# GNN with a mixture of experts on one Trainium2 core: the first 14 slices of the adjacency build among the preparation

## Chip, cores and metric

One Trainium2 chip (trn2), one of its NeuronCores. The metric is the device time of one execution in microseconds (us), and the number compared is the median of several runs.

## What is computed

The input is `x`, 3125 nodes of 256 features, and 53125 directed edges (25000 drawn pairs in both directions, one self loop per node), sorted by destination. It goes through a graph network and a mixture of experts, each with a residual:

```python
h = layernorm(x)
for _ in range(6):                                   # six steps
    r = maximum(h @ W1.T + b1, 0)
    msg = segment_sum((r @ W2.T + b2)[src], dst)     # over 53125 edges
    xr, xz, xn = split(msg @ W_ih.T + b_ih)          # GRU cell
    hr, hz, hn = split(h @ W_hh.T + b_hh)
    z = sigmoid(xz + hz)
    h = (1 - z) * tanh(xn + sigmoid(xr + hr) * hn) + z * h
x = x + h
y = layernorm(x)
logits = y @ Wg + bg + bias                          # 8 experts, the best 2
x = x + sum over the two of weight * (relu(y @ F1[e] + fb1[e]) @ F2[e] + fb2[e])
```

## The kernel before, in words

**Data.** The segment sum is a product with the dense adjacency matrix `adj`, 25 tiles of 128 source nodes by 3136 destination columns in fp8, which stays in SBUF. States and ReLU outputs are kept as a high and a low fp16 part (`x_hi`, `x_lo`; `r_hi`, `r_lo`), and the gate weights too (`wht`, `wct`; the latter is W_ih times W2, one product less in each step).

**Preparation.** The edges come sorted in blocks of 64. VectorE turns them into keys and rows; TensorE transposes them and spreads the lowest and highest destination of each block over the partitions (`diag`, `lim_b`). From these VectorE works out for each slice of 16 columns the first block (`bnd[.., 0]`) and the last block (`bnd[.., 1]`) (L643 to L653); the first goes on to `slot_key` and `picked` and a product on TensorE (L1473) that fetches each slice's edges as three slots of 128. The last block serves only the question whether a slice has more edges than three slots hold (`more`, and `bound` with its two DMAs), which decides the `slow_flag`. With it set, `redo` code and exact steps run on every engine, in branches that are skipped otherwise; these inputs skip them. Then come the statistics of x (L675, L678), `rstd` as a power on GpSimd (L503), x normalised on VectorE (L735), its transposes on TensorE with their halves made by ScalarE and VectorE (`state_part`, 13 of them), W1, the product W_ih times W2 (L1514), and eight transposes of scaled gate weights (L1530).

**Build.** `adj` has 196 slices in 7 turns of 28. For each slice VectorE compares (`hots`, L889 and L895: one `hot_row` for two slices, three `hot_key`), TensorE multiplies (`slice_sums`, L1637: three matmuls into one of two banks), ScalarE evicts to fp8 (`evict`, L1280) and GpSimd copies two slices into `adj` (L506). A turn ends with the node degrees (L1645). The engines each run their own written order. What they do between the slices stands in the functions `beside(w, b)`, where b is the slice's place in its turn: turn 0 holds the first nine ReLU sums of step 0 (b = 0, 3, 6 ...), turn 1 four more and the first messages, later turns messages and gates of the window of the turn before. VectorE may be four slices ahead of TensorE (`DEEP`).

**Steps.** Step 0 is fused into the build. Then TensorE reads the flag and runs steps 1 to 4 in a loop and step 5 written out, seven windows of up to 512 columns each: messages (L1587), gates (L1611); a step's last window shares its time with the next step's ReLU sums (`step_end`). At the start of step 1 ScalarE issues the DMAs that reload x and the router's weights for the tail (L1344 to L1351), as soon as GpSimd has cleared `x1` (L515).

**Experts.** The tail adds the residual, normalises, chooses the experts and scatters rows of 260 floats to `slot_in` in DRAM; an expert loop over tiles of 256 rows multiplies, and GpSimd adds each result to `out` with an indirect DMA (L591). At the end of each expert GpSimd waits for its two DMAs (L595, L596, the `tock` operations).

**The order around the change.** All orders are written by hand, with semaphores. Until now no slice starts before the eighth weight transpose and the last state part are done (L1535 to L1537). The lines that set the place of a slice in the preparation, for TensorE:

```python
pe.wait_ge(sem("w_lo"), 9)
pe.wait_ge(sem("slot_tables"), 1)
pe.wait_ge(sem("state_lo"), NW)
...
for g in range(NSL):
    slice_sums(g)
    beside(g // GROUP - 1, g % GROUP)
```

## Time and profile before

| | |
|---|---|
| median of 3 runs | 1967.47 us (1966.49 to 1970.06) |
| the profiled execution's own time | 1965.98 us |
| its span in the trace | 1964.2 us |
| busy share of the span | TensorE 93%, its weight loads 56%, VectorE 56%, ScalarE 31%, GpSimd 17% |
| mean granted TensorE clock | 0.969 of full speed |
| instructions | 30148 |

All engine times below are counted from the start of the span. PE is TensorE, PEld its weight loads, DVE VectorE, ACT ScalarE, POOL GpSimd, SP SyncE. A granted clock of 1.0 is 2.4 GHz, 0.5 is 1.2 GHz. "128x512 f16<-128x512 f32" is partitions by elements of output and input. In brackets stands how long an engine was idle before an instruction, and what ended the wait; "issue" means that the engine waited for nothing that the profile shows. A duration in a timeline can overlap with the next one's start; the cost of an instruction in a full queue is the distance of two starts.

### The profile page before, as it was taken

The numbers are of one execution on the slowest core, as the hardware profiler recorded it, in microseconds if no ns is written. First come the engines' busy times: TensorE is split into PE (matmuls) and PEld (weight loads), VectorE is DVE, ScalarE is ACT, GpSimd is POOL, SyncE is SP. The second block draws the span as 40 slices with busy tenths as digits, with TensorE's granted clock in tenths as the row PEclk, the third lists the DMA queues.
The fourth block names the chain that finished last, engine by engine and source line by source line (L and its number), as shares of the span: only waits on it lengthen the run. The fifth ranks groups of instructions, "written<-read, shape, count | busy, mean of one in ns | idle before, by whom it ended". The sixth has DMA issues, their size and how long they took to land.

```text
span 1964.2 us, 30148 instructions
## 1 busy us (share of the span) xinstructions
PE 1825.1 (93%) x10716; PEld 1097.3 (56%) x10717; DVE 1103.2 (56%) x2622; ACT 608.8 (31%) x1254; POOL 337.3 (17%) x454
## 2 busy tenths in 40 slices
PE   2789999999999999999999999999999999839996
PEld 1555555555444574445744457444574456629996
DVE  6897888875144562344624446244452556736775
ACT  0154444434112242122411224122241112216663
POOL 1011111100455500000000000000000013234665
PEclk7799999999999999999999999999999999959998
DMA  8940000000443300000000000000000011564543
GB/s 265 336 158 2 1 2 2 1 2 2 166 133 133 129 23 1 1 1 1 2 1 1 1 1 2 1 1 1 1 1 1 12 44 56 218 247 73 87 74 52
DMA packets 74505, 109.64 MB, mean 56 GB/s; under 512 B 12334, under 2 KB 65369, under 8 KB 73076
## 3 DMA queue, kind: packets, MB, share of 16 engines
q1 hardware_dynamic: 51086, 49.57, 8.1%
q0 software_dynamic: 18368, 38.09, 7.7%
q10 hardware_dynamic: 4902, 20.01, 2.6%
q8 instruction: 92, 1.51, 0.3%
q14 instruction: 57, 0.47, 0.1%
HBM read 43.59 MB, written 65.05 MB: 55 GB/s over the span
## 4 chain that ended last, share of the span: by engine, by line
PE 72%; issue 14%; POOL 7%; DVE 5%; ACT 1%; DMA 0%; POOLq 0%; SPq 0%; ACTq 0%; DVEq 0%
PE bank L1587 36%; PE bank L1611 25%; PE bank L1562 5%; PE bank L1637 4%; POOL out L591 3%; POOL slot_in L568 2%; POOL tick L590 1%; DVE hot_key L895 1%; PE bank L1473 1%; ACT stage L1280 1%; DVE xa L735 0%; DVE hot_row L889 0%; POOL rstd L560 0%; PE bank L1514 0%; DMA out<-slot_y,dest 0%
## 5 line engine op out<-in xcount | busy, mean ns | idle before, releaser
L1587 PE MATMUL bank<-adj,r_hi 128*128 128x512 fp8e4 (+4 forms) x2100 | 731.1, 353 | 0.0
L1587 PE MATMUL bank<-adj,r_lo 128*128 128x512 fp8e4 (+4 forms) x2016 | 703.3, 353 | 0.0
L1587 PEld LDWEIGHTS bank<-adj,r_hi 128*128 128x128 f16 x2100 | 205.9, 98 | 188.4 <-issue 1.9
L1587 PEld LDWEIGHTS bank<-adj,r_lo 128*128 128x128 f16 x2016 | 197.6, 98 | 179.8 <-issue 1.9
L792 DVE SCALAR_TENSOR_TENSOR m_lo<-bank,msg_unit,m_hi 128x512 f16<-128x512 f32 (+4 forms) x84 | 57.2, 682 | 283.4 <-ACT m_hi L1210 283.1
L1611 PE MATMUL bank<-x_hi,wht_hi 128*128 128x512 f16 (+4 forms) x504 | 177.3, 352 | 0.5 <-DVE m_lo L792 0.5
L1611 PE MATMUL bank<-m_hi,wct_lo 128*128 128x512 f16 (+4 forms) x504 | 177.3, 352 | 0.0
L1611 PE MATMUL bank<-x_hi,wht_lo 128*128 128x512 f16 (+4 forms) x504 | 177.3, 352 | 0.0
L1611 PE MATMUL bank<-m_lo,wct_hi 128*128 128x512 f16 (+4 forms) x504 | 177.3, 352 | 0.0
L1611 PE MATMUL bank<-m_hi,wct_hi 128*128 128x512 f16 (+4 forms) x504 | 177.3, 352 | 0.0
L1611 PE MATMUL bank<-x_lo,wht_hi 128*128 128x512 f16 (+4 forms) x504 | 177.3, 352 | 0.0
L1210 ACT ACTIVATE m_hi<-bank,msg_unit 128x512 f16<-128x512 f32 (+4 forms) x84 | 53.1, 632 | 352.3 <-PE bank L1587 352.3
L895 DVE TENSOR_SCALAR hot_key<-iota_key,slot_key 128x400 f16<-128x400 f16 x588 | 156.5, 325 | 0.0
L1280 ACT ACTIVATE stage<-bank 128x400 fp8e4<-128x400 f32 x196 | 98.5, 504 | 153.9 <-PE bank L1637 147.2
L1637 PE MATMUL bank<-hot_key,hot_row 128*128 128x400 f16 x588 | 126.8, 334 | 12.4 <-DVE hot_key L895 7.1
L555 POOL MEMSET x_rows<- 128x4 f32 (+1 forms) x3 | 0.2, 97 | 793.1 <-PE bank L1794 793.1
L1217 ACT ACTIVATE gate_a<-gate_a,gate_bias,gate_unit 128x512 f32<-128x512 f32 (+4 forms) x84 | 63.7, 759 | 228.5 <-DVE gate_a L808 228.5
L1221 ACT ACTIVATE gate_a<-gate_a,gate_bias,gate_unit 128x512 f32<-128x512 f32 (+4 forms) x84 | 63.6, 757 | 150.4 <-DVE gate_a L822 150.4
L811 DVE SCALAR_TENSOR_TENSOR gate_z<-degree,deg_w,bank 128x512 f32<-128x512 uint16 (+4 forms) x84 | 56.8, 676 | 89.2 <-PE bank L1611 89.2
L506 POOL COPY adj<-stage 128x200 uint32<-128x200 uint32 x98 | 46.7, 477 | 319.8 <-ACT stage L1280 319.8
L591 POOL DMA_INDIRECT out<-slot_y,dest x58 | 90.9, 1568 | 20.5 <-issue 14.4
L785 DVE SCALAR_TENSOR_TENSOR r_lo<-bank,r_hi 128x512 f16<-128x512 f32 x72 | 49.2, 689 | 80.4 <-ACT r_hi L1204 79.4
(298 smaller groups left out, 2878.9 us busy)
## 6 DMA issues: line engine op xcount, KB each, us to landing
slot_in<-fill_rows SPq DMA_DIRECT2D x2, 13520.0 KB, 68.9
ffn_scratch<-pair POOLq DMA_DIRECT2D x32, 512.0 KB, 3.2
ffn_w<-ffn_scratch ACTq DMA_DIRECT2D x8, 2048.0 KB, 18.8
x_rows<-in_L_ffn_W POOLq DMA_DIRECT2D x32, 256.0 KB, 4.0
slot_x<-slot_in SPq DMA_DIRECT2D x30, 260.0 KB, 3.1
xa<-in_x SPq DMA_DIRECT2D x1, 3072.0 KB
x<-in_x ACTq DMA_DIRECT2D x1, 3072.0 KB
out<-x SPq DMA_DIRECT2D x4, 512.0 KB
```

The lines of the kernel that those rows point to most:

```text
L591: pool.indirect_dma_start(out[:], bass.IndirectOffsetOnAxis(ap=dest[j][:, 0:1], axis=0), slot_y[j][:], None, bounds_check=N - 1, oob_is_er ...
L792: v.scalar_tensor_tensor(m_lo[:, w % 2, f, 0:n], bank[f][:, 0:n], msg_unit[:, 0:1], m_hi[:, w % 2, f, 0:n], ALU.mult, ALU.subtract)\
L811: ins = v.scalar_tensor_tensor(z, dg, deg_w[:, 2 + f:3 + f], bank[5][:, 0:n], ALU.mult, ALU.add)
L895: last = v.tensor_scalar(hot_key[k][:], iota_key[:], slot_key[:, g, s:s + 1], None, ALU.is_equal)
L1210: a.activation(m_hi[:, w % 2, f, 0:n], bank[f][:, 0:n], ACT.Copy, scale=msg_unit[:, 0:1]).then_inc(sem(again + "msg_hi"), 1)
L1217: a.activation(gate_a[:, 0:n], gate_a[:, 0:n], ACT.Sigmoid, bias=gate_bias[:, f:f + 1], scale=gate_unit[:, f:f + 1]).then_inc(acts, 1)
L1221: a.activation(gate_a[:, 0:n], gate_a[:, 0:n], ACT.Tanh, bias=gate_bias[:, 4 + f:5 + f], scale=gate_unit[:, 4 + f:5 + f]).then_inc(acts, 1)
L1280: a.activation(stage[g // 2 % 2][:, :, (b % 2) * SW:(b % 2 + 1) * SW], bank[2 + (g + i) % RING][:, 0:NT * SW].rearrange("p (q c) -> p q c" ...
L1562: last = mm(o[:, k * D:(k + 1) * D], xs[:, t, n0:n0 + P], ws[:, t, :], start=False, stop=True, skip_group_check=True)
L1587: last = mm(bank[f][:, 0:n], r[:, q, f * P:(f + 1) * P], c, start=q == 0 and i == 0, stop=q == NT - 1 and i == len(todo) - 1)
L1611: last = mm(bank[b][:, 0:n], wgt, mov, start=i == 0, stop=i == len(todo) - 1)
L1637: last = mm(bank[2 + (g + i) % RING][:, 0:NT * SW], hot_row[b // 2 % 2][:, b % 2, s, :], hot_key[k][:], start=s == 0, stop=s == SLOTS - 1)
```

## The change

1. **Slices in the preparation** (`AHEAD = 14`). Slices 0 to 13 are built between the state parts and the weight transposes, in the written orders of TensorE, VectorE and ScalarE. As `adj` lies over memory that the preparation still uses, their evictions go to seven buffers of their own (`early_stage`), which GpSimd copies once states and weights are done. The state parts use banks 0 and 1 instead of 2 and 3, the transposes of W_hh wait for the three scaled parts of wc and for `deg_w`.
2. **ReLU sums of turn 0** stand at slices 14, 16, 17, 19, 20, 22, 23, 25, 26 instead of 0, 3, ... 24, and their low parts four slices later.
3. **x is normalised by ScalarE** with scale `rstd` and bias `shift`, a new VectorE operation behind `rstd`: twelve tiles ahead of W1's copies, the others among the slices.
4. **Out of VectorE's head**: the copies to `key_t`, `row_t` and of the upper limits go to ScalarE; the last blocks (`last_block`) go behind slices 56 and 57, `bound` and `more` (`bounds`) behind slice 58. `block_id` and `mask` are fp16 now, one mask for each half.
5. **SyncE** sends the bounds after the seven `adj` copies of the twin rows, and it issues the reload DMAs, once in the slow branch and once in a new branch for the common case.
6. **TensorE's branches**: the redo code moves into the slow branch of the steps, and the common branch stands first.
7. **GpSimd** waits for the last output DMAs once, after the last expert, instead of after each.

The diff, cut to its core (a line of dots stands for what is left out: what only moved along, or is told in the list):

```diff
+X_FIRST = 12
+AHEAD = 14
+RELU_AT = (14, 16, 17, 19, 20, 22, 23, 25, 26)
@@ SyncE @@
+            for w in range(TURNS):
...
             sp.wait_ge(sem("bound_col"), 1)
...
-            for w in range(TURNS):
+            def reload():
+                sp.wait_ge(sem("x1_clear"), 1)
...
+            with sp.If(slow < 1):
+                reload()
@@ GpSimd @@
             for p in range(NSL // 2):
+                if p == 0:
+                    pool.wait_ge(sem("state_lo"), NW)
+                    pool.wait_ge(sem("w_lo"), 9)
                 pool.wait_ge(sem("stage_full"), 2 * p + 2)
...
-                for j in range(TT):
-                    pool.wait_ge(sem(f"y_out{j}"), pool.snap(pool.snap(done) * 16 + 16))
-                    pool.tensor_tensor(tock[:, e * TT + j:e * TT + j + 1], valid[:], valid[:], ALU.mult).then_inc(sem("expert_sent"), 1)
+            for j in range(TT):
+                pool.wait_ge(sem(f"y_out{j}"), pool.snap(pool.snap(done) * 16 + 16))
+                pool.tensor_tensor(tock[:, j:j + 1], valid[:], valid[:], ALU.mult).then_inc(sem("expert_sent"), 1)
@@ VectorE @@
+            dve.wait_ge(sem("rstd_ready"), 1)
+            v.scalar_tensor_tensor(shift[:], mv[:, :, 0], -1.0, rstd[:], ALU.mult, ALU.mult).then_inc(sem("shift_ready"), 1)
             v.memset(ones_h[:], 1.0)
...
-            for t in range(NT):
-                v.tensor_scalar(xa[:, t, :], xa[:, t, :], mv[:, t, 0:1], rstd[:, t:t + 1], ALU.subtract, ALU.mult)\
-                 .then_inc(sem("x_norm"), 1)
...
+            def last_block(t):
+                link(v.scalar_tensor_tensor(mask[t][:, 0:NB], block_id[:, 0:NB], 1.0, mask[t][:, 0:NB], ALU.add, ALU.mult))
+                link(v.tensor_reduce(bnd[:, t, 1:2], mask[t][:, 0:NB], AX.X, ALU.max))
...
+                if w == 1 and b in (0, 1):
+                    last_block(b)
+                if w == 1 and b == 2:
+                    bounds()
...
+            hots(0)
...
+            state_part(0)
+            for u in range(1, X_EARLY):
+                state_part(u)
+                hots(u)
+            for c in range(3):
+                dve.wait_ge(sem("wc_sums"), c + 1)
+                v.tensor_reduce(peak[:, 1, 2 * c:2 * c + 2], bank[4 + c][:].rearrange("p (o j) -> p o j", o=2), AX.X, ALU.max, apply_absolute_value=True).then_inc(sem("peaks"), 1)
+                hots(X_EARLY + c)
...
+            hots(X_EARLY + 3)
             for i, wt in enumerate((wht, wct)):
                 for j in range(4):
...
+                    if X_EARLY + 4 + 4 * i + j < AHEAD:
+                        hots(X_EARLY + 4 + 4 * i + j)
-            for g in range(NSL):
+            for g in range(AHEAD, NSL):
@@ ScalarE @@
+            def normalise(t):
+                a.activation(xa[:, t, :], xa[:, t, :], ACT.Identity, bias=shift[:, t:t + 1], scale=rstd[:, t:t + 1]).then_inc(sem("x_norm"), 1)
+            act.wait_ge(sem("shift_ready"), 1)
+            for t in range(X_FIRST):
+                normalise(t)
...
+            state_part(0)
+            state_part(1)
+            for u in range(2, X_EARLY):
+                evict(u - 2)
+                normalise(X_FIRST + 2 * (u - 2))
+                normalise(X_FIRST + 2 * (u - 2) + 1)
+                state_part(u)
...
+                    if X_EARLY + 2 + 4 * i + j < AHEAD:
+                        evict(X_EARLY + 2 + 4 * i + j)
...
-            act.wait_ge(sem("stage_free"), NSL // 2)
-            act.wait_ge(sem("x1_clear"), 1)
@@ TensorE @@
+            state_part(0)
+            for u in range(1, X_EARLY):
+                state_part(u)
+                slice_sums(u - 1)
...
             for c in range(3):
...
                 last.then_inc(sem("wc_sums"), 1)
+                slice_sums(X_EARLY - 1 + c)
...
+                    pe.wait_ge(sem("deg_w_done"), 1)
...
+                    if X_EARLY + 2 + 4 * i + j < AHEAD:
+                        slice_sums(X_EARLY + 2 + 4 * i + j)
...
-            with pe.If(slow > 0):
+            def redo_first():
...
-            with pe.If(slow > 0):
-                all_steps(True)
             with pe.If(slow < 1):
                 all_steps(False)
+            with pe.If(slow > 0):
+                redo_first()
+                all_steps(True)
```

## Rows read from the trace of the kernel before

**Rows 1.** Stretches: us, each engine's busy time (instructions), PEclk, DMA share, GB/s.

```profile
66.90:82.90 16.00, 4.70 (x24) 3.84 (x25) 13.58 (x36) 3.14 (x6) 0.00 (x0) 0.68 1.09 336
...
91.70:105.50 13.80, 9.68 (x58) 8.51 (x57) 11.88 (x26) 7.36 (x16) 0.00 (x0) 0.75 1.10 336
105.50:142.30 36.80, 32.00 (x214) 20.55 (x215) 34.53 (x115) 19.61 (x65) 6.32 (x14) 0.95 0.39 142
```

**Rows 2.** VectorE in the table chain, timeline and groups by shape.

```profile
24.75 2.22 DVE L639 COPY lim_b<-bank 128x512 f32<-128x512 f32 x4 [2.16 <-PE bank L1460]
...
L651 DVE SCALAR_TENSOR_TENSOR e_f<-block_id,mask 128x831 f32<-128x831 f32 x2 | 2.0, 1025 | 0.1
L652 DVE TENSOR_REDUCE bnd<-e_f 128x1 f32<-128x831 f32 x2 | 2.0, 1019 | 0.1
...
40.19 0.17 DVE L655 CAST bound<-bnd 128x4 int32<-128x4 f32 x1
```

**Rows 3.** rstd on GpSimd and what VectorE does then; the x normalisation.

```profile
57.13 4.36 POOL L503 TENSOR_TENSOR rstd<-rstd,expo 128x25 f32<-128x25 f32 x1 [50.90 <-DVE rstd L680]
...
60.85 0.17 DVE L700 MEMSET ones_h<- 128x128 f16 x1
...
L735 DVE TENSOR_SCALAR xa<-xa,mv,rstd 128x256 f32<-128x256 f32 x25 | 8.2, 405 | 0.0
```

**Rows 4.** ScalarE, timeline at 1707 us: start, duration, operation.

```profile
1707.69 0.65 ACT L1217 ACTIVATE gate_a<-gate_a,gate_bias,gate_unit 128x310 f32<-128x310 f32 x1 [3.71 <-DVE gate_a L808]
1708.24 0.63 ACT L1219 ACTIVATE gate_z<-gate_z,gate_bias,gate_unit 128x310 f32<-128x310 f32 x1
```

**Rows 5.** VectorE, timeline in turn 0: two slices' keys, relu_lo, hot_row.

```profile
114.52 1.48 DVE L895 TENSOR_SCALAR hot_key<-iota_key,slot_key 128x400 f16<-128x400 f16 x6
115.92 0.68 DVE L785 SCALAR_TENSOR_TENSOR r_lo<-bank,r_hi 128x512 f16<-128x512 f32 x1
116.52 0.65 DVE L889 TENSOR_TENSOR hot_row<-iota_row,turn_row 128x768 f16<-128x768 f16 x1
```

**Rows 6.** TensorE, timeline in turn 0: one slice, one ReLU sum, two slices.

```profile
111.97 0.68 PE L1637 MATMUL bank<-hot_key,hot_row 128*128 128x400 f16 x3 [0.18 <-ACT stage L1280]
112.48 0.38 PE L1557 MATMUL bank<-b_rows,ones_h 128*128 128x256 f16 x2
...
114.01 1.18 PE L1637 MATMUL bank<-hot_key,hot_row 128*128 128x400 f16 x6
```

**Rows 7.** TensorE, timeline: four transposes of x in the preparation.

```profile
97.11 1.06 PE L1484 MATMUL bank<-ident,xa 128*128 128x128 f32 x4
```

**Rows 8.** Line 506: durations in ns, least, median, most.

```profile
L506 POOL COPY adj<-stage x98: 356/357/1078, 112.0 to 427.6; 128x200 uint32<-128x200 uint32 x98
```

**Rows 9.** Turn 2's start, timelines of VectorE and TensorE.

```profile
185.28 0.67 DVE L792 SCALAR_TENSOR_TENSOR m_lo<-bank,msg_unit,m_hi 128x448 f16<-128x448 f32 x1
...
187.21 0.35 PE L1611 MATMUL bank<-x_hi,wht_hi 128*128 128x448 f16 x1
```

**Rows 10.** TensorE after steps 0 and 1, timelines; and the stretch between.

```profile
493.19 0.18 PE L1731 MATMUL bank<-ones_h 128*128 128x2 f16 x1 [6.35 <-issue]
...
493.61 0.63 PE L1587 MATMUL bank<-adj,r_lo 128*128 128x512 fp8e4 x1
494.04 0.63 PE L1587 MATMUL bank<-adj,r_hi 128*128 128x512 fp8e4 x1
...
738.75 0.17 PE L1731 MATMUL bank<-ones_h 128*128 128x2 f16 x1 [1.59 <-issue]
...
494.00:496.00 2.00, 2.00 (x6) 0.76 (x5) 0.02 (x1) 0.00 (x0) 0.00 (x0) 0.50 0.05 12
```

**Rows 11.** The end: TensorE before the last columns; VectorE's last slot_y, GpSimd's tick.

```profile
1717.60 1.41 PE L1759 MATMUL bank<-ident,x_rows 128*128 128x128 f32 x6 [4.73 <-DVE x_rows L1042]
...
1951.02 0.34 DVE L1146 TENSOR_SCALAR slot_y<-y_sum,share 128x256 f32<-128x256 f32 x1
...
1952.74 0.19 POOL L590 TENSOR_TENSOR tick<-valid 128x1 f32<-128x1 f32 x1
```

More of the change, by code:

```diff
@@ L189, in gnn_ffn @@
         at_messages = used[0]
+        early_scope = ExitStack()
+        yb = allocator(early_scope)
+        early_stage = [yb(f"early_stage{p}", [P, NT, 2 * SW], F8) for p in range(AHEAD // 2)]
+        skip_to(yb, "to_gate_z", at_messages + 5 * DT * 1024)
+        mask = [yb("mask0", [P, CG * P], F16)]
+        skip_to(yb, "to_x_new", at_messages + 6 * DT * 1024)
+        block_id = yb("block_id", [P, CG * P], F16)
+        mask.append(yb("mask1", [P, CG * P], F16))
+        early_end = used[0]
+        early_scope.close()
         m_hi = ss("m_hi", [P, 2, DT, 512], F16)
@@ L196, in gnn_ffn @@
         at_build = used[0]
+        assert edge_end <= at_messages + 5 * DT * 1024 and early_end <= at_build
         bs = ExitStack()
@@ L357, in columns_of, with staged @@
             return (FUSED_LEN[w], FUSED_COL[w]) if fused else (WIN_LEN[w], WIN_COL[w])
+        def staged(p):
+            return early_stage[p] if p < AHEAD // 2 else stage[p % 2]
         def ring_free(engine, item):
@@ L628, in _ @@
             last.then_inc(sem("diags"), 1)
-            dve.wait_ge(sem("keys_t"), 1)
-            for i, table in ((0, key_t), (1, row_t)):
-                for h in range(2):
-                    last = v.tensor_copy(table[:, h * 2 * P:(h + 1) * 2 * P], bank[2 * i + h][:].rearrange("p (c two) -> p c two", two=2)[:, :, 0])
-            last.then_inc(sem("edge_table"), 1)
             dve.wait_ge(sem("lims_b"), 1)
-            for m in range(2):
-                for h in range(2):
-                    n = min(4, CG - 4 * h) * P
-                    last = v.tensor_copy(lim_b[:, m, h * 512:h * 512 + n], bank[4 + 2 * m + h][:, 0:n])
+            for h in range(2):
+                n = min(4, CG - 4 * h) * P
+                last = v.tensor_copy(lim_b[:, 0, h * 512:h * 512 + n], bank[4 + h][:, 0:n])
             link(last)
@@ L870, in step_end, with bounds @@
                 state_lo(s, NW - 1)
+            def last_block(t):
+                link(v.scalar_tensor_tensor(mask[t][:, 0:NB], block_id[:, 0:NB], 1.0, mask[t][:, 0:NB], ALU.add, ALU.mult))
+                link(v.tensor_reduce(bnd[:, t, 1:2], mask[t][:, 0:NB], AX.X, ALU.max))
+            def bounds():
+                link(v.tensor_copy(bound[:], bnd[:]))
+                link(v.tensor_scalar(bound[:, :, 1], bound[:, :, 1], 1, None, ALU.add))
+                v.tensor_scalar(bound[:], bound[:], 1, None, ALU.arith_shift_right).then_inc(sem("bound_col"), 1)
+                for t in range(SL_T):
+                    link(v.scalar_tensor_tensor(more[:, t:t + 1], bnd[:, t, 1:2], float(-2 * SLOTS), bnd[:, t, 0:1], ALU.add, ALU.subtract))
             def hots(g):
@@ L898, in beside @@
             def beside(w, b):
-                if w == -1 and b % 3 == 1 and b >= 4:
-                    relu_lo(b // 3 - 1, b // 3 - 1, first=True)
-                if w == 0 and b == 0:
-                    relu_lo(RELU_BUILD - 1, RELU_BUILD - 1, first=True)
+                if w <= 0 and b - 4 + (GROUP if w == 0 else 0) in RELU_AT:
+                    u = RELU_AT.index(b - 4 + (GROUP if w == 0 else 0))
+                    relu_lo(u, u, first=True)
+                if w == 1 and b in (0, 1):
+                    last_block(b)
+                if w == 1 and b == 2:
+                    bounds()
                 if w == 0 and b in (4, 6, 8, 10):
@@ L1184, in state_part @@
                     a.activation(x_hi[:, :, TWIN_COL + TWIN:NPAD], xt[:, :, 0:TWIN], ACT.Copy).then_inc(sem("xt_hi"), 1)
+            act.wait_ge(sem("keys_t"), 1)
+            for i, table in ((0, key_t), (1, row_t)):
+                for h in range(2):
+                    last = a.activation(table[:, h * 2 * P:(h + 1) * 2 * P], bank[2 * i + h][:].rearrange("p (c two) -> p c two", two=2)[:, :, 0], ACT.Copy)
+            last.then_inc(sem("edge_table"), 1)
+            act.wait_ge(sem("lims_b"), 1)
+            for h in range(2):
+                n = min(4, CG - 4 * h) * P
+                last = a.activation(lim_b[:, 1, h * 512:h * 512 + n], bank[6 + h][:, 0:n], ACT.Copy)
+            last.then_inc(sem("lim_high"), 1)
+            def normalise(t):
[3 more added lines that the diff above has]
+                normalise(t)
             act.wait_ge(sem("w_tr"), 1)
@@ L1286, in beside @@
             def beside(w, b):
-                if w == -1 and b % 3 == 1:
-                    relu_hi(b // 3, b // 3, first=True)
+                if w == -1 and b - 1 in RELU_AT:
+                    relu_hi(RELU_AT.index(b - 1), RELU_AT.index(b - 1), first=True)
                 if w == 0 and b in (1, 3, 5, 7):
@@ L1648, in beside @@
             def beside(w, b):
-                if w == -1 and b % 3 == 0 and b // 3 < RELU_BUILD:
-                    relu_sum(FIRST, b // 3)
+                if w == -1 and b in RELU_AT:
+                    relu_sum(FIRST, RELU_AT.index(b))
                 if w == 0 and b in (0, 2, 4, 6):
```

219 lines of the change are left out of this document (106 added, 113 removed).

## The prediction

> **What bounds the kernel now.** I read the page first; its shares are an average that hides the start, so the second view is the busy time by stretch [rows 1]. It shows a kernel of two kinds. From about 142 us on TensorE is the bound nearly everywhere. Ahead of that it is not: from 66.9 to 82.9 us it is busy 4.7 of 16.0 us at a granted clock of 0.68 (part of it at 1.2, part at 2.4 GHz), from 91.7 to 105.5 us 9.7 of 13.8 at 0.75, while VectorE works nearly throughout (13.6 and 11.9). From 105.5 to 142.3 us, the first turn of 28 slices with nine ReLU sums, both are nearly full (32.0 and 34.5 of 36.8). The third view, the timelines, gives the price of one piece. The reader is to see that the first 142 us are a chain through VectorE with holes on TensorE, and that turn 0 could use those holes if its pieces fit.
>
> **The table chain, ahead of the slices.** The two upper-limit copies of lim_b leave VectorE, half of the four that take 2.22 us: -1.1. The last-block product and reduction (L651, L652, two each) go to turn 2: 4 x 1.02 = -4.1. Five small bound operations of 0.17 us go with them: -0.9 [rows 2]. The key copies moved to ScalarE lay in a wait for TensorE and give nothing. Against that VectorE now waits for rstd ahead of L700, which it reached at 60.85 us while GpSimd ended at 57.13 + 4.36 = 61.49 [rows 3]: 0.6 plus one 0.2 us operation, of which 0.3 lies beside the 16.7 us of slot sums: +0.5. The slot tables stand at 61.3 instead of 66.9 us: **-5.6**. x must have landed 6 us earlier; its statistics waited for no DMA, and I take it that it has.
>
> **x normalised by ScalarE.** 25 operations, 8.2 us, leave VectorE [rows 3]; in their place stands slice 0's one-hots (turn_row 0.3, hot_row and three keys 1.2): -8.1 + 1.5 = **-6.6** on VectorE's chain. On ScalarE an operation with scale and bias from memory started 0.55 us after its like at 310 columns [rows 4]; for 256 I take 0.50. Twelve take 6.0 us from 55.6 us, so the copies of w1 and W_ih begin at 61.6; they end ahead of x's first transposes' eviction at about 64.2, which VectorE wants only at 65.7. Hidden, with 1.5 us to spare. The other 13 are 6.5 us spread over a ScalarE that was busy 3.1 of 16.0 us [rows 1].
>
> **Slices 1 to 13 inside the preparation.** A slice costs VectorE 0.7 us for three keys (six in 115.92 - 114.52 = 1.40) and, every second one, about 0.55 for hot_row (0.65 busy): 1.0 on average [rows 5]. It costs TensorE 0.51 us at the full clock (112.48 - 111.97) and a ReLU sum 1.53 (114.01 - 112.48) [rows 6]; at the half clock a slice is 1.0. Four x transposes are busy 1.06 at the half clock [rows 7], 0.85 from one group to the next. Followed along the in-order queues:
> Rounds 1 to 5: one-hots, slice sums, eviction plus two normalisations, x copy, x_lo. Two rounds fit in one loop of 0.15 + 1.0 + 0.2 + 0.5 + 1.0 + 0.6 + 0.6 + 0.7 = 4.8 us, so 2.4 a round; before, the loop is transposes, copy, x_lo and two hand-overs, 0.85 + 0.6 + 0.6 + 0.4 = 2.45 for two, 1.2 a round: +5.8.
> The three gate-weight products: three slices on TensorE and four on VectorE, partly beside each other, and the transposes now wait for all of wc and for deg_w (0.25 us later): +2.8.
> The eight weight transposes: VectorE pays 0.95 for each of four slices, cold TensorE some of two: +4.3.
> Together **+12.9**, 1.0 us a slice: VectorE's own price, since it seldom waits. The preparation ends at 105.5 - 5.6 - 6.6 + 12.9 = 106.2 us. Between ends: with TensorE at the full clock the rounds shrink to 1.6 (VectorE's 0.6 + 1.0) and a slice to 0.6 (-5); with every hand-over exposed see the slower rival; +6 is my bound for the range.
>
> **The rest of turn 0.** The kernel before spends 36.8 us on 28 slices and nine ReLUs. Left are 14 slices and nine ReLUs: 14 x 0.51 + 9 x 1.53 + 0.5 for the degree sum = 21.4; VectorE has 14 + 9 x 0.6 + 1.1 = 20.5, so TensorE bounds it. Add 1.6 before the first slice, 1.5 for a cold start (both as before) and 1.0 of ring waits: 25.5. **-11.3**. GpSimd may not copy before the weights and states are done, so seven copies stand in one burst. Their row says 0.36 median and 1.08 longest [rows 8]: 2.5 to 7.6 us, against some 7 until eviction 18 wants the eighth. The Trainium skill (SBUF — State Buffer, Who interferes with whom) says a VectorE operation in a two-port mode locks GpSimd out for its whole length; if all seven met it, the sum would be 1 us worse. I take 0 and keep +1.
>
> **Turns 1 and 2.** Turn 1 gets one more x-part product (relu_lo) on VectorE: **+0.5**. Turn 2 gets what left the head: last_block twice and bounds, 5.0 us of VectorE between slices 56 and 58 and ahead of msg_lo. The nearest rows: msg_lo, the last of that run, ends at 185.95 us, and the first gate sum, which needs it, starts at 187.21 [rows 9]. Only 1.3 us of cover against 5.0: **+3.7**. Lower bound 0, if VectorE is ahead of its time by then; upper +7, if the gap drops the clock too.
>
> **The branch after step 0.** TensorE stood 6.35 us before its first message of step 1, released by "issue", with every ReLU long done; at the end of the next step the same line waits 1.59. After the 6.35 it ran at a granted clock of 0.50, 1.2 GHz, its matmuls 0.43 us apart [rows 10]. TensorE jumped there over the redo code and over the exact steps. Now the common path falls through. I leave it 1.3 us: -5.05. Without that stall I expect the clock to stay, as 14 matmuls at 0.427 against 0.213 us: -2.95. Next is the ReLU of tile 20: its sums come after 40 messages, 8.5 us, within which the last x_lo is written. **-8.0**. The Trainium skill (Runtime: NRT & Kernel Launch, Instruction fetch mechanics) says that a taken branch out of the current window waits for a DMA fetch of its target. By that rule a jump is merely moved: it now stands after the last step. There TensorE waits 4.73 us for x2_norm anyway [rows 11], against some 3 us (half of 6.35) for a jump. The sum takes it as hidden.
>
> **Reload DMAs on SP.** TensorE was never idle while ScalarE issued them, but with it 8 us earlier they would have held the ReLU of tile 20; on SP nothing does. SP's queue: the bounds now go behind the seven adj copies, the last of them at the end of the build, and are wanted only for the slow flag, a window's messages and gates later; x1_clear is the same event as before. POOL's queue is passed by nothing else. 0.
>
> **The expert loop.** TensorE bounds it; only the end shows. slot_y was ready at 1951.4 us (1951.02 + 0.34), GpSimd ticked at 1952.74, held by two tocks [rows 11]: **-1.2**, bounds -2 and 0.
>
> **Sum.** -5.6 - 6.6 + 12.9 - 11.3 + 0.5 + 3.7 - 8.0 - 1.2 = -15.6 us. The profiled execution took 1965.98 us (span 1964.2), 1.5 below the median of the runs, 1967.47. 1965.98 - 15.6 + 1.5 = 1951.9, said as 1952.
>
> **Rivals.** (A) The branch gives nothing: the 6.35 us are something else, a register load, say. For it: I saw no row of a fetch. Against: ScalarE, with one jump, lost little, TensorE with two lost most, and 1.59 us stand where there is none. 1952 + 8 = 1960. Chance 0.11.
> (B) Slower: the slices don't fill holes but lengthen the chain. Place: the rounds and the weight loop. Price: 1.2 VectorE + 1.0 cold TensorE + 0.5 ScalarE + 0.4 of hand-overs = 3.1 us a slice instead of 1.0, 13 x 2.1 = +27: 1979. It decides once a slice costs 2.2 us (1.0 + 15.6 / 13). Against: one-hots run up to four slices ahead of TensorE, and TensorE's holes are there [rows 1]. Chance 0.05.
> (C) The lump in turn 2 drops the clock and turn 2 stays behind: +7 instead of +3.7, and GpSimd's burst of copies holds the eviction, +1: 1956. For it: a hole of 2.9 us ahead of slice 0 was followed by the half clock. Chance 0.10.
> (D) The jump behind the last step isn't hidden but costs its 3 us: 1955. The trace gives 4.7 us of cover. Chance 0.03.
> (E) The overlap is only half of it: a slice costs 2.0 us in the preparation, +13: 1965, no change. Chance 0.03.
> Forecast 0.68, its own range 1945 to 1958.
>
> **Numbers.** The range takes in A and C and the better bound: 1943 to 1961. A measurement can tell 0.2%, 3.9 us. Faster: forecast, A, C, D = 0.92; same: E = 0.03; slower: B = 0.05.
>
> **What will show it.** The page of after: last weight copy near 106 us, degree sum of turn 0 near 131 (142 before); a hole of 3 to 4 us on TensorE at slice 58; the first matmul of the steps within 2 us of the last gate sum, at clock 1.0; x_hi copies no later than VectorE wants them. A preparation that ends beyond 112 us, or the 6.35 us still there, makes me wrong.

## The result, and the profile after

| | before | changed |
|---|---|---|
| median | 1968.53 us (4 runs, 1966.49 to 1970.06) | 1953.17 us (4 runs, 1951.42 to 1955.50) |
| the profiled execution | 1965.98 us, span 1964.2 | 1951.86 us, span 1950.1 |
| ratio of the runs | | 0.9922, 95% interval 0.991 to 0.9935 |
| mean granted clock | 0.969 | 0.972 |

The kernel is 0.8% faster; 1952 us was forecast. Between the two profiled executions lie 14.1 us (15.6 forecast). A ledger shows where, by marks that exist in both traces: each row is what the stretch took before and after, and the last row is their sum.

| stretch | before | after | measured | forecast |
|---|---|---|---|---|
| start to the slot tables' end | 66.88 | 62.11 | -4.8 | -5.6 |
| from there to the first `x_lo` | 11.06 | 4.43 | -6.6 | -6.6 |
| to the last weight copy (preparation) | 27.04 | 37.99 | +10.9 | +12.9 |
| to the degree sum of turn 0 | 36.59 | 25.61 | -11.0 | -11.3 |
| turn 1 | 42.66 | 42.65 | 0.0 | +0.5 |
| turn 2 | 48.23 | 54.00 | +5.8 | +3.7 |
| turns 3 to 6 | 194.13 | 194.12 | 0.0 | 0 |
| last degree sum to TensorE's mark of step 2 | 312.16 | 302.25 | -9.9 | -8.0 |
| to the wait for `x_rows` | 978.85 | 979.31 | +0.5 | 0 |
| expert loop, to `ended` | 240.87 | 241.89 | +1.0 | -1.2 |
| sum | | | -14.1 | -15.6 |

("TensorE's mark" is the two-column matmul of L1731, L1793 after, with which a step begins.)

VectorE's timeline of the changed kernel at the marks of the head; the first row has its counterpart in [rows 2], the third in [rows 3]:

```profile
25.73 1.16 DVE L667 COPY lim_b<-bank 128x512 f32<-128x512 f32 x2 [4.14 <-PE bank L1519]
...
56.38 0.19 DVE L722 SCALAR_TENSOR_TENSOR shift<-mv,rstd 128x25 f32<-128x25 f32 x1 [0.64 <-POOL rstd L535]
...
62.11 0.25 DVE L869 CAST turn_row<-slot_row 128x168 f16<-128x168 f32 x1
```

Two copies, 1.16 us together, stand where four, 2.22 us together, stood, and the wait for `rstd` is 0.64 us. The next view is the busy time by stretch, as [rows 1] (columns: stretch, its length, busy us and count of each engine, granted clock, DMA share, GB/s): the five rounds of states, the gate-weight products, the weight transposes, the rest of turn 0.

```profile
core 0: us, PE busy (x) PEld busy (x) DVE busy (x) ACT busy (x) POOL busy (x), PEclk, DMA share, GB/s
66.50:79.70 13.20, 8.21 (x40) 5.21 (x39) 8.54 (x25) 10.60 (x26) 0.00 (x0) 0.89 1.09 336
79.70:87.60 7.90, 7.90 (x48) 6.71 (x46) 5.80 (x20) 2.76 (x8) 0.00 (x0) 0.91 1.09 335
87.60:104.50 16.90, 11.69 (x72) 8.58 (x71) 15.59 (x41) 10.18 (x28) 0.00 (x0) 0.80 1.09 335
104.50:130.90 26.40, 23.26 (x171) 17.41 (x171) 21.73 (x65) 11.74 (x36) 5.25 (x13) 0.94 0.58 211
```

In the rounds ScalarE is the fullest engine, not VectorE; in the weight transposes VectorE is nearly full. TensorE's timeline shows the start of the rest of turn 0, the degree sums of turns 0 and 1 and the start of turn 2, where a gate matmul took 0.35 us in [rows 9]:

```profile
107.61 0.67 PE L1661 MATMUL bank<-hot_key,hot_row 128*128 128x400 f16 x3 [3.78 <-DVE hot_key L887]
...
130.14 0.73 PE L1669 MATMUL bank<-deg_hot,ones_h 128*128 128x448 f16 x3
...
172.79 0.74 PE L1669 MATMUL bank<-deg_hot,ones_h 128*128 128x448 f16 x3 [0.24 <-ACT stage L1326]
...
178.30 1.16 PE L1661 MATMUL bank<-hot_key,hot_row 128*128 128x400 f16 x3 [2.62 <-DVE hot_key L887]
179.68 0.56 PE L1635 MATMUL bank<-x_hi,wht_hi 128*128 128x448 f16 x1 [0.22 <-DVE m_lo L773]
```

The hole at slice 58 is there (2.62 us), and behind it a gate matmul takes 0.56 to 0.58 us instead of 0.35 until 183.4 us: the granted clock is at its lower level, 1.2 GHz. This text calls that the half clock. At the end of step 0 nothing is left of the hole of [rows 10]:

```profile
480.81 0.35 PE L1635 MATMUL bank<-m_hi,wct_lo 128*128 128x438 f16 x1
480.99 0.17 PE L1793 MATMUL bank<-ones_h 128*128 128x2 f16 x1
481.02 0.38 PE L1611 MATMUL bank<-adj,r_hi 128*128 128x512 fp8e4 x1
```

The chain of work that ended last is as before, 72% TensorE and 14% issue.

### The profile page after: what moved, and what is told of

Same layout as the page of the kernel before. It is cut to its first block, busy times and chain, and to the rows that moved or that the text cites. A ratio compares the mean times of both kernels' runs of the same rounds, so it can differ in the third digit from the quotient of the medians.

```text
span 1950.1 us, 30119 instructions
## 1 busy us (share of the span) xinstructions
PE 1826.3 (94%) x10716; PEld 1100.3 (56%) x10717; DVE 1094.6 (56%) x2592; ACT 622.1 (32%) x1285; POOL 332.6 (17%) x440
## 4 chain that ended last, share of the span: by engine, by line
PE 72%; issue 14%; POOL 7%; DVE 4%; ACT 1%; DMA 1%; POOLq 1%; SPq 0%; ACTq 0%; DVEq 0%
PE bank L1611 36%; PE bank L1635 25%; PE bank L1586 5%; PE bank L1661 4%; POOL out L626 3%; POOL slot_in L603 2%; POOL tick L625 1%; DMA out<-slot_y,dest 1%; DVE hot_key L887 1%; ACT stage L1326 0%; DVE st L696 0%; ACT xa L1236 0%; POOL rstd L595 0%; PE bank L1697 0%; DVE x_lo L746 0%
## 5 line engine op out<-in xcount | busy, mean ns | idle before, releaser
L1326 ACT ACTIVATE stage<-bank 128x400 fp8e4<-128x400 f32 x182 | 91.4, 503 | 156.9 <-PE bank L1661 151.5
L1661 PEld LDWEIGHTS bank<-hot_key,hot_row 128*128 128x128 f16 x588 | 56.3, 99 | 69.7 <-issue 16.8
L1906 PE MATMUL bank<-xt_hi,ffn_w 128*128 128x256 f32 x464 | 91.2, 290 | 4.3 <-DVE xt_lo L1155 4.3
```

The source lines that it names most:

```text
L1326: a.activation(staged(g // 2)[:, :, (b % 2) * SW:(b % 2 + 1) * SW], bank[2 + (g + i) % RING][:, 0:NT * SW].rearrange("p (q c) -> p q c", c ...
L1661: last = mm(bank[2 + (g + i) % RING][:, 0:NT * SW], hot_row[b // 2 % 2][:, b % 2, s, :], hot_key[k][:], start=s == 0, stop=s == SLOTS - 1)
L1906: last = mm(bank[h][:, 0:TILE], f1w(e, i, t, h), xs[:, t, :], start=k == 0, stop=k == 5)
```

## The experiments

Eleven kernels ran, each timed in five rounds against the kernel before; the stretches are those of the ledger, from the profiled execution. The last stretch is the one from the last degree sum to the mark of step 2.

| kernel | median us | ratio (95%) | turn 0 ends | turn 1 | turn 2 | last stretch |
|---|---|---|---|---|---|---|
| before (profile) | | 1 | 141.57 | 42.66 | 48.23 | 312.16 |
| changed | 1953.17 | 0.9922 (0.9910 to 0.9935) | 130.14 | 42.65 | 54.00 | 302.25 |
| before, branch alone | 1967.67 | 1.0004 (0.9995 to 1.0012) | 141.49 | 42.66 | 48.23 | 311.21 |
| before, reload alone | 1968.51 | 1.0003 (0.9994 to 1.0013) | 141.13 | 42.67 | 48.22 | 311.84 |
| before, both | 1958.59 | 0.9952 (0.9939 to 0.9966) | 141.19 | 42.65 | 48.23 | 302.59 |
| changed, branch back | 1958.25 | 0.9963 (0.9950 to 0.9977) | 129.31 | 42.65 | 53.42 | 310.32 |
| changed, bounds spread | 1946.58 | 0.9897 (0.9883 to 0.9912) | 129.66 | 43.96 | 48.22 | 302.69 |
| changed, no slices ahead | 1952.77 | 0.9927 (0.9912 to 0.9941) | 131.78 | 44.31 | 54.34 | 302.78 |
| changed, ten ahead | 1953.40 | 0.9934 (0.9921 to 0.9948) | 130.89 | 42.65 | 52.95 | 302.55 |
| changed, x on VectorE | 1954.67 | 0.9932 (0.9919 to 0.9945) | 137.09 | 42.65 | 54.10 | 302.25 |
| changed, ReLU first | 1950.68 | 0.9910 (0.9894 to 0.9925) | 127.21 | 42.65 | 54.25 | 302.53 |
| changed, ReLU first and bounds spread | 1941.67 | 0.9874 (0.9859 to 0.9889) | 128.10 | 42.65 | 48.23 | 302.73 |
| before, tocks once | 1966.60 | 0.9993 (0.9984 to 1.0002) | 142.68 | 42.66 | 48.23 | 312.04 |

Five of these kernels have the same code up to the end of turn 0 (before, branch alone, reload alone, both, tocks once), and it ends at 141.13 to 142.68: one profiled start is good to some 0.8 us either way. The turns repeat to 0.1 us where no clock change falls into them. The two long stretches behind the table do not: from the mark of step 2 to the wait for `x_rows` the thirteen profiles take 978.9 to 980.5 us, and the expert loop takes 238.3 to 244.2. The intervals of two kernels, each against the kernel before, leave some 3.5 to 4 us of uncertainty between the two; where less is read below, it is read from the traces.

**1. The branch alone, in the kernel before.**

```diff
-            with pe.If(slow > 0):
+            def redo_first():
...
-            with pe.If(slow > 0):
-                all_steps(True)
             with pe.If(slow < 1):
                 all_steps(False)
+            with pe.If(slow > 0):
+                redo_first()
+                all_steps(True)
```

> The kernel before with one edit: TensorE falls through to the common steps, and the repair of step 0 stands in the other branch. Everything else, ScalarE's reload included, is as before. The forecast priced this at -8.0 us (stall of 6.35 us down to 1.3, and 2.95 us of half-clock matches gone); rival A says 0, since the wait would return under another name. The two profiles say more than the forecast: between the last degree sum and step 1's first match the offset goes from -5.7 to -15.6, so -9.9. Theory: 1956 us profiled (1966.0 - 9.9), ratio 0.995, the first match after step 0 within 0.5 us of the last gate sum and at full clock. Rival A: 1966, ratio 1.000. If only the reload's move to SyncE made the stall go, this run keeps it too.

Measured: 1.0004, no gain at all, and not for rival A's reason. TensorE's and ScalarE's timelines of this kernel:

```profile
486.60 0.17 PE L1731 MATMUL bank<-ones_h 128*128 128x2 f16 x1
...
509.09 0.40 PE L1562 MATMUL bank<-w1t_hi,x_hi 128*128 128x256 f16 x1 [6.73 <-ACT bank L1242]
```

```profile
497.03 0.45 ACTq L1346 DMA_DIRECT2D x<-in_x  x1
497.52 5.29 ACTq L1347 DMA_DIRECT2D x<-in_x  x1
502.83 2.43 ACTq L1348 DMA_DIRECT2D wg<-in_L_ffn_Wg  x1
505.29 0.56 ACTq L1349 DMA_DIRECT2D bg_b<-in_L_ffn_bg  x1
505.88 0.72 ACTq L1350 DMA_DIRECT2D bg_b<-in_L_ffn_bias  x1
506.63 0.45 ACTq L1351 DMA_DIRECT2D x_rows<-in_L_ffn_b  x1
507.29 0.60 ACT L1204 ACTIVATE r_hi<-bank 128x512 f16<-128x512 f32 x1 [13.37 <-issue]
```

The hole of 6.35 us is gone: step 1 begins at 486.60 with no wait. The DMA view says what the hole was. It has a queue for instructions, and in the kernel before it shows two packets of 16 KB in it between 486.8 and 493.2 us, the hole:

```profile
q8 instruction: 2, 0.03, 3.4%
```

They run from 488.69 to 491.15 us. The four profiled kernels that keep the old branch (before, reload alone, branch back, tocks once) each have two such packets inside the hole; in the nine others there is none in the 6.4 us before that mark. But 15.8 us later TensorE stops, for 6.73 us, before the ReLU of tile 20, whose bank ScalarE fills, and ScalarE is busy issuing the six reload DMAs from 497.03 to 507.08, 10.05 us, 5.29 of them for one instruction. Nearly all that was won goes there, and to the clock: the last stretch shrinks by only 0.95 us.

**2. The reload alone, in the kernel before:** the six DMAs, and the branch around them, go from ScalarE's to SyncE's order.

> The kernel before with one edit: the six reload DMAs are issued by SyncE instead of ScalarE; TensorE keeps its branch. The piece to look at is the stretch from the last degree sum to the two-column mark of step 2: 312.16 us before, 311.21 with the branch alone, 310.32 with the changed kernel's branch undone, 302.25 changed. Theory (the two edits need each other): ScalarE's issue ran beside TensorE's 8.5 us of messages that nobody waited behind, so this edit alone is worth at most 2 us: stretch 310 to 312, ratio 0.999 to 1.000, the 6.35 us wait on issue still there. Rival: the reload's place is worth the gain by itself and the branch only the rest: stretch 305 or less, ratio 0.996.

Measured: 1.0003, the stretch 311.84, the wait on issue still 6.37 us:

```profile
492.77 0.18 PE L1735 MATMUL bank<-ones_h 128*128 128x2 f16 x1 [6.37 <-issue]
```

The first theory holds: in the kernel before, the late TensorE hid the issuing.

**3. Both, in the kernel before.**

> The kernel before with both edits, TensorE's fall-through and the reload on SyncE, and nothing else of the change. Theory: together they give the whole 9.9 us (the stretch from the last degree sum to step 2's mark 302.3 us), 1956 us profiled, ratio 0.995; the wait of 6.7 us for ScalarE's bias fill ahead of the ReLU of tile 20, which the branch alone had, is gone. Rival: something else in the changed kernel (the late bounds, the turns' shift) is needed as well; then the stretch stays above 308 us and the ratio above 0.998.

Measured: 0.9952, -9.4 us, the stretch 302.59. The waits list of this kernel has the mark with which a step begins at 4.1 us in three waits, those of the later steps, the longest 1.5:

```profile
PE bank L1735 <- issue: 4.1, 3, 1.5
```

It has no wait of L1566, its ReLU line, for ScalarE's fill. Two edits that are worth nothing each are worth 9.4 us together. That is also most of the 15 us of the whole change: what is left for the rest of the list is 0.9922 against 0.9952, some 6 us.

**4. The branch undone, in the changed kernel.**

> The changed kernel with that one edit undone: TensorE tests the flag and jumps over the repair of step 0 again. Theory: the 6.35 us wait on issue and the half clock come back, +9.9 us, 1961.8 us in the profiled run, ratio 0.997. Rival A: nothing comes back, 1951.9, ratio 0.992. Lying between (+5 to +7) would mean that the reload, now issued by SyncE, carried a part of the gain.

Measured: 0.9963, the stretch 310.32, and the hole is back:

```profile
485.74 0.18 PE L1793 MATMUL bank<-ones_h 128*128 128x2 f16 x1 [5.99 <-issue]
```

The stretch is 8.1 us longer than the changed kernel's (310.32 - 302.25), and the ratios say the same, 0.0041 of 1967 us. The 9.9 expected of it was too much: the hole is 0.36 us shorter than before, and so is the half clock behind it, by some 1.5 us: from 490 us on the granted clock is 1.00, against 0.58 from 495 to 500 in the kernel before.

**5. The bounds spread over turn 1, in the changed kernel.**

```diff
-                if w == 1 and b in (0, 1):
-                    last_block(b)
-                if w == 1 and b == 2:
+                if w == 0 and b in (19, 21):
+                    last_block((b - 19) // 2)
+                if w == 0 and b == 23:
                     bounds()
```

> The changed kernel with the last-block search and the bounds (12 small VectorE operations, some 5 us) taken out of the first three slots of turn 2 and put in the slots of slices 19, 21 and 23 of turn 1. Between the degree sums of turn 1 and turn 2 the offset to the kernel before went from -11.44 to -5.7, that is 5.7 us for the lump and the half clock behind it. Theory: TensorE's queue covers VectorE in the later slots of turn 1, so some 5 us come back: 1947 us profiled, ratio 0.990 against before, the hole of 2.6 us at slice 58 gone and its gate sums at 0.35 us from the first. Rival: VectorE is just as short of time there, the hole only moves; 1951 to 1952.

Measured: 0.9897, 4.9 us better than the changed kernel (some 3.8 of uncertainty). Turn 2 is back at 48.22, and turn 1 pays 1.3 us, for one new hole of 1.10 us:

```profile
161.36 0.67 PE L1661 MATMUL bank<-hot_key,hot_row 128*128 128x400 f16 x3 [1.10 <-DVE hot_key L887]
```

It stands behind slice 19, where VectorE was late already: msg_lo waits there for ScalarE, and both kernels have a standing hole of 1.89 us just before.

**6. No slices ahead, in the changed kernel:** the calls of `hots`, `slice_sums` and `evict` in the preparation are taken out (left out here), and the ReLU sums go back to every third slice.

```diff
-AHEAD = 14
-RELU_AT = (14, 16, 17, 19, 20, 22, 23, 25, 26)
+AHEAD = 0
+RELU_AT = (0, 3, 6, 9, 12, 15, 18, 21, 24)
```

> The changed kernel with no slice ahead: all 28 slices of turn 0 behind the preparation and a ReLU every third slice as before; the tables, ScalarE's normalisation, the late bounds and the branch stay as changed. The forecast's terms are +12.9 us in the preparation and -11.3 in the rest of turn 0, so the overlap itself would be worth -1.6, i.e. this run would be about 1.6 us faster than the changed kernel. Its trace has 38.5 us from the first low half of the states to the end of the preparation (27.5 before) and 25.9 from there to the end of turn 0 (36.8 before), a sum of 0.1. Theory: within 2 us of the changed kernel, 1950 to 1954, ratio 0.992. Rival: the preparation before was partly held by VectorE's and ScalarE's other work, so that the slices filled idle time and are worth 5 us or more: 1957 or above, ratio 0.995 or more.

Measured: 0.9927 against 0.9922. The time doesn't tell them apart. The marks do, a little: the preparation from the first `x_lo` takes 28.2 us instead of 38.0, the rest of turn 0 37.6 instead of 25.6. The overlap costs 9.8 and gives 12.0, 2.2 us; slice 0's one-hots, 0.7 us ahead of the first `x_lo`, are not in that sum, so that the overlap is worth some 1.5 us. My terms made it a loss of 1.6, the rival a gain of 5. The slices ahead, the headline of the change, are one of its smallest parts. Another 1.66 us of this kernel lie in turn 1 and are the clock's. Rows of the kernel without slices ahead, its timeline and then its stretches:

```profile
159.50 1.86 PE L1649 MATMUL bank<-hot_key,hot_row 128*128 128x400 f16 x6 [1.89 <-DVE hot_key L887]
161.15 0.58 PE L1599 MATMUL bank<-adj,r_hi 128*128 128x448 fp8e4 x1
```

```profile
160.00:165.00 5.00, 4.97 (x20) 2.24 (x19) 3.88 (x15) 1.55 (x5) 0.55 (x1) 0.66 0.01 2
```

The same hole of 1.89 us stands in the changed kernel at 157.86, and there the clock stays at 1.00.

**7. Ten slices ahead instead of 14.**

> The changed kernel with 10 slices ahead instead of 14: the four slices in the weight transposes go back to turn 0. By the forecast they cost VectorE 4 x 0.95 = 3.8 us there (4.3 in all), and a slice in turn 0 costs TensorE, which bounds it, 0.51 us and VectorE 1.0. With every 28 slices ahead of none the degree sum of turn 0 came at 131.8 us, with 14 at 130.1. Theory (VectorE pays for a slice wherever it stands, so the place changes little): preparation ends some 4 us earlier, at about 101 us, and the degree sum of turn 0 stands within 1.5 us of 130.1; time within 2 us of the changed kernel, ratio 0.992. Rival: the four filled holes of TensorE and ScalarE, and turn 0 pays the full price of an even slice of the kernel before (36.8 / 28 = 1.3 us each): degree sum at 133 or later, ratio 0.994.

Measured: 0.9934, turn 0 ends at 130.89. From the scaling of `whn` to the last weight copy it takes 15.5 us, where the six kernels with 14 ahead take 16.9 to 17.4: the last four slices cost 1.4 to 1.9 us there, not 3.8, while the rest of turn 0 is 28.1 us instead of 25.6. The theory "within 1.5 us" holds for the mark, which is 0.75 us later; this profile also started 0.7 us earlier (slot tables at 61.41 instead of 62.11), so that ten ahead cost some 1.5 us. The reason given for the theory, that a slice costs VectorE the same anywhere, does not hold. Here it costs 0.35 to 0.5 us, and in the rest of turn 0 it costs 0.6.

**8. x normalised by VectorE, in the changed kernel:** ScalarE's normalisations and `shift` are taken out (left out here).

```diff
             dve.wait_ge(sem("slot_tables"), 1)
+            dve.wait_ge(sem("rstd_ready"), 1)
+            for t in range(NT):
+                v.tensor_scalar(xa[:, t, :], xa[:, t, :], mv[:, t, 0:1], rstd[:, t:t + 1], ALU.subtract, ALU.mult)
             hots(0)
```

> The changed kernel with x normalised by VectorE again, 25 operations (8.2 us by the row of the kernel before) between the slot tables and slice 0's one-hots; ScalarE does none. Theory of the forecast: they stand on VectorE's chain, which bounds the preparation, so they come back less what VectorE now waits there: its first low half of the states starts at 66.5 us with slice 0's one-hots ahead of it; some 6.6 us, degree sum of turn 0 at 136 to 137 instead of 130.1, ratio 0.995 to 0.996. Rival: ScalarE was the slower place in the rounds (a normalisation there takes longer, and it also evicts), so that VectorE doing them costs 3 us or less: degree sum at 133 or earlier, ratio 0.993 or less.

Measured in the trace: turn 0 ends at 137.09, 7.0 us later, as the theory says. The first `x_lo` is 8.0 us later (74.52), and the rounds give 1.4 to 2.4 us back, 11.7 us instead of 13.1 to 14.1, because ScalarE has less to do there. Measured in the time: 0.9932 against 0.9922, 2 us with some 3.6 of uncertainty, so less than 7. The profiled execution is 7.4 us behind at the wait for `x_rows` and only 3.8 at `ended`. Most of the difference, 2.6 of 3.6 us, is one spot, the first tiles of the expert loop. VectorE's second and third tile, of the changed kernel:

```profile
1753.53 0.69 DVE L1155 TENSOR_TENSOR xt_lo<-bank,xt_hi 128x512 fp32r<-128x512 f32 x1
...
1761.40 0.69 DVE L1155 TENSOR_TENSOR xt_lo<-bank,xt_hi 128x512 fp32r<-128x512 f32 x1 [7.03 <-ACT xt_hi L1466]
```

and of this one:

```profile
1760.87 0.69 DVE L1157 TENSOR_TENSOR xt_lo<-bank,xt_hi 128x512 fp32r<-128x512 f32 x1
1766.17 0.69 DVE L1157 TENSOR_TENSOR xt_lo<-bank,xt_hi 128x512 fp32r<-128x512 f32 x1 [4.46 <-ACT xt_hi L1459]
```

7.87 us against 5.30. TensorE's clock there differs, and that is why (first the changed kernel, then this one, at the same place of the loop):

```profile
1755.00:1760.00 5.00, 5.00 (x25) 5.00 (x25) 0.00 (x0) 1.47 (x4) 0.00 (x0) 0.50 0.19 53
```

```profile
1762.00:1767.00 5.00, 5.00 (x43) 4.87 (x43) 0.83 (x4) 3.08 (x8) 0.00 (x0) 1.00 0.22 53
```

Each kernel has one profile, so whether this one has the better clock there in every execution is not shown, and why its median is nearer than its trace stays open to that extent.

**9. The first ReLU sum ahead of slice 14.**

```diff
+            relu_sum(FIRST, 0)
             for g in range(AHEAD, NSL):
                 slice_sums(g)
...
-                if w == -1 and b in RELU_AT:
+                if w == -1 and b in RELU_AT[1:]:
                     relu_sum(FIRST, RELU_AT.index(b))
```

> The changed kernel with one edit on TensorE: the first ReLU sum of turn 0 goes ahead of slice 14's sums instead of behind them, so that TensorE has work while VectorE makes the degree one-hots and slice 14's one-hots (TensorE waits 3.78 us there and then runs its next 13 matmuls at twice their time). Theory: TensorE bounds the rest of turn 0 (it has no wait between 107.6 and 130.1 us), so the first ReLU sum's 1.5 us leave the chain, and with a shorter hole part of the 2 us of the half clock: -2 to -4 us, degree sum of turn 0 at 126 to 128, 1948 to 1950, ratio 0.991. Rival: VectorE is as full as TensorE there and sets the end: the degree sum stays at 130.

Measured: 0.9910, 2.4 us better than the changed kernel by the ratios, which is within their uncertainty; the trace has it, as the rest of turn 0 takes 23.5 us instead of 25.6. TensorE's timeline:

```profile
104.29 0.39 PE L1581 MATMUL bank<-b_rows,ones_h 128*128 128x256 f16 x2 [1.31 <-DVE wct_lo L950]
...
106.75 0.67 PE L1661 MATMUL bank<-hot_key,hot_row 128*128 128x400 f16 x3 [0.77 <-DVE hot_key L887]
```

The hole of 3.78 us is down to 1.31 and 0.77, with 0.31 and 0.50 at the next two slices, 0.9 us less in all. The other part is the clock: from 104 to 112 us it is 1.00 here, and in the changed kernel it is 0.61 from 107.61 to 112.

**10. Both improvements together,** with the three pieces in the slots of slices 13, 24 and 26 of turn 1.

> The changed kernel with the first ReLU sum ahead of slice 14 (degree sum of turn 0 at 127.2 us instead of 130.1 when alone) and with the last-block search and bounds in turn 1, now in the slots of slices 13, 24 and 26 instead of 19, 21 and 23 (where they cost 1.3 us of turn 1 and saved 5.8 of turn 2). Theory: the two add up, -2.9 - 4.5, and the better slots, one of which is a wait of 2.0 us of VectorE for TensorE, give back most of the 1.3 us: turn 1 takes 42.7 to 43.2 us, turn 2 48.2, two-column mark of step 2 at 715.5 us instead of 723.2, time 1945 us, ratio 0.988. Rival: with the ReLU first, VectorE has no slack left in turn 1 and the operations cost their 5 us there: turn 1 above 45 us, ratio 0.9895 or more.

Measured: 1941.67 us, 0.9874 (0.9859 to 0.9889), turn 1 at 42.65, turn 2 at 48.23, the mark of step 2 at 715.85. The better slots give back the whole 1.3 us: one piece of 2.0 us lies in a wait of VectorE for TensorE, the others behind the standing hole, where VectorE runs ahead. This version is 1.3% faster than the kernel before, 0.5% faster than the changed one.

**11. The tocks once, in the kernel before.**

> The kernel before with one edit: GpSimd waits for the scatters and writes its tocks once behind the last expert, not behind each. The forecast gave -1.2 us, all of it at the last slot, where GpSimd ticked 1.72 us after slot_y's first write; the changed kernel's tick comes 0.44 after. Theory: 0.4 to 0.5 us there, about -1.3 us, ratio 0.9993 (the two middle experts' tocks stand beside TensorE's work), which is at the edge of what five rounds can tell. Rival: nothing, ratio 1.000, as the time of the second slot of the expert loop alone varies by 2.7 us from kernel to kernel (5.2 to 7.9 us).

Measured: 0.9993, which fits -1.3 us and also nothing. The traces tell more. From the start of TensorE's last matmul to that of `ended` the four kernels with the old waits take 10.7 to 10.8 us and this one 9.3; the changed kernel and the seven built on it take 8.3 to 9.4. The place is the tick behind the last tile's first `slot_y` write. In the changed kernel's GpSimd timeline, beside [rows 11], with that write at 1938.22:

```profile
1938.66 0.18 POOL L625 TENSOR_TENSOR tick<-valid 128x1 f32<-128x1 f32 x1 [0.78 <-DVE slot_y L1184]
```

It comes 0.44 us behind the write, and 0.43 in this kernel (1955.70 and 1956.13), where the kernel before has 1.72.

## Why the prediction was right, step by step

**The table chain (-5.6, measured -4.8).** The removed work is what I said: from the first `lim_b` copy to `slot_key` it took 18.1 us and takes 12.0 (37.70 - 25.73), -6.1 as forecast. But the first copy started at 25.73 instead of 24.75, behind TensorE, 1.0 us that I had no term for. Some half of it is this profile's start and no part of the change: over the changed kernel and the seven built on it that copy starts at 24.80 to 25.87, 25.3 in the mean, over the kernel before and the four built on it at 24.72 to 25.36, 24.9 in the mean. By the means of those kernels in which the mark can be read (seven and five) the slot tables are 5.4 us earlier, near the 5.6. The wait for `rstd` was 0.64, as worked out.

**x by ScalarE (-6.6, measured -6.6).** Experiment 8 gives 7.0 for it in the trace. "Hidden" was too strong for the rounds: ScalarE is busy 10.6 of 13.2 us there, and without the normalisations they take 1.4 to 2.4 us less. The price of one was right: twelve took 6.01 us, 0.50 each.

**Slices in the preparation (+12.9, measured +10.9).** By parts, before and over the five kernels with 14 ahead and x on ScalarE: the rounds 8.6 and 13.1 to 14.1 us (forecast +5.8), the gate-weight products 5.1 and 7.2 to 8.0 (forecast +2.8), the weight transposes 13.3 and 16.9 to 17.4 (forecast +4.3). The term that was mis-sized is the price of 1.0 us a slice, "VectorE's own price, since it seldom waits": with no slices ahead the three parts take 9.3, 5.1 and 13.8 us, 28.2 in all, so 13 slices cost 9.8 us, 0.75 each. VectorE did wait, in the rounds for ScalarE (it is busy 8.5 of 13.2 us), and part of its slices lay there. That speaks against rivals B and E: a slice was never near 2 us.

**The rest of turn 0 (-11.3, measured -11.0).** 25.6 us against 25.5 worked out. From the end of the last weight copy to the first slice it takes 2.5 us (107.61 - 105.08), the end of the hole of 3.78, where I had 1.6: the degree one-hots now fall between the preparation and slice 14. The ring waits of 1.0 us didn't come. The seven copies took 3.10 us, 0.44 each instead of 0.36, and beside them VectorE's six keys took 1.95 us from start to start (106.41 to 108.36) instead of 1.40 [rows 5]. By the rule of the Trainium skill (SBUF — State Buffer, Who interferes with whom) a VectorE instruction in a two-port mode and a GpSimd one wait for the whole of each other; the two rows, slower on both engines, fit that, though no row here says in which mode the keys ran. It cost VectorE half a microsecond inside the 3.78, and no eviction waited.

**Turn 1 (+0.5, measured 0.0).** The product that I added lay where VectorE had time to spare, and the stretch is 42.65 to 42.67 us in eleven of the thirteen kernels.

**Turn 2 (+3.7, measured +5.8).** The size was off, in rival C's direction. TensorE's holes at the turn's start are 0.27, 0.53, 2.62 and 0.22 us where they were 0.27 and 0.26, so +3.1: the term as forecast was near that. The rest is the half clock: slice 58's three matmuls 0.5 us longer, and eleven gate matmuls 0.19 us longer each, 2.1 us. The step that failed is the clock, which I left at its full level in this term. Over the six kernels that have the lump the turn took 52.95 to 54.34 us. GpSimd's burst, the other half of C, did not add.

**The branch (-8.0, measured -9.9).** Near in size, wrong in how it was told. The stall went entirely (from 6.35 us to none, where I left 1.3), the half clock with it. "Reload DMAs on SP: 0" is only the order of counting: the text says that ScalarE would have held tile 20's ReLU if TensorE came earlier, and experiments 1 to 3 show that this is all of it, 6.73 us and a clock drop of their own. Rival A, that the wait is something else and the branch gives nothing, is refuted: experiment 1 keeps the flag's read and loses the wait, and experiment 3 turns that into time. The prediction knew of no row of a fetch; the instruction packets inside the hole, shown under experiment 1, are that row. The Trainium skill (Runtime: NRT & Kernel Launch, Instruction fetch mechanics) makes a taken branch, whose target lies outside the window at hand, pay for the fetch of it; the rows agree, 6.35 us with two jumps and none with a fall-through. By that rule the jump now stands behind the last step; TensorE's wait for `x_rows` is 4.74 us there, 4.73 before, so it is hidden, and rival D has nothing.

**The expert loop (-1.2, measured +1.0).** The last slot gave its 1.3 us, and experiment 11 has it in its own trace. The loop ahead of it lost 2.3, of which 1.5 is the third tile's clock, 7.87 us against 6.36. That is no part of the change: over the kernels here that distance was 5.20 to 7.88 us. The whole loop, to `ended`, took 238.3 to 243.5 us in the changed kernel and the seven built on it, and 240.9 to 244.2 in the kernel before and the four built on it, so one pair of profiles can't tell this stretch to 2 us.

**What was to show it.** Last weight copy near 106 us (104.5), degree sum near 131 (130.1), a hole of 3 to 4 us at slice 58 (2.62, and 0.53 ahead of it), the steps' first matmul within 2 us of the last gate sum at full clock (at once): these came. One sign failed: the `x_hi` copies were to be no later than VectorE wants them, and VectorE waits for them twice in the rounds, 1.01 and 1.46 us:

```profile
69.53 0.69 DVE L746 TENSOR_TENSOR x_lo<-bank,x_hi 128x512 f16<-128x512 f32 x1 [1.01 <-ACT x_hi L1219]
...
74.33 0.69 DVE L746 TENSOR_TENSOR x_lo<-bank,x_hi 128x512 f16<-128x512 f32 x1 [1.46 <-ACT x_hi L1219]
```

The errors of +0.8, -2.0, +2.1, -1.9 and +2.2 us nearly cancelled. That the total is better than its parts is luck.

## What to carry to other kernels

A stall is worth its length only if the next engine in line is ready that much earlier: ask what each queue does in the time you win, and move that too, or two edits look worthless one by one that are worth 9.4 us together. Work moved off a crowded engine's chain should be cut up and put into slots where that engine waits; in one lump at the start of a turn it cost 5.8 us, in three pieces at waits nothing. Filling holes of one engine is worth little when another engine pays the same work: 14 slices ahead gave 1.5 to 2 us, for the most intricate part of the change.

## What was not expected of the hardware

The same hole of 1.89 us on TensorE in turn 1 left the granted clock at 1.00 in one kernel and dropped it to the half clock in another, at a price of 1.66 us. After the hole of 9.4 us ahead of the expert loop, and shorter ones of 1.50 and 2.81 us up to 1754.4, the changed kernel's TensorE had 0.84 of its clock from 1750 to 1755 us, 0.50 again to 1760 and 0.96 after that, though it was busy throughout from 1755; between two kernels with the same code there the third tile came 5.20 and 7.87 us behind the second. So one profiled execution of a kernel with holes carries some 2 to 3 us that belong to no edit, and in the expert loop of this one up to 5. And six plain DMAs held the engine that issued them for 10.05 us, 5.29 of it in the second of them, a piece of 53 KB, behind one of 3072 KB: issuing is not free for an engine that others wait for.
